# Attention score rows from one stationary block: high and low weights side by side, their two groups of rows added afterwards

## The reference

```
feats   = x W                       (8 heads of 64 units)
e_self  = feats . a_self            e_neigh = feats . a_neigh      (per head and node)
dense   = leaky_relu(e_self[i] + e_neigh[j], 0.2), only where adj[i, j] = 1
x1      = layernorm(x + relu(softmax(dense) feats + b))
agg     = adj x1 / max(row sum of adj, 1e-6)
out     = layernorm(x1 + relu([x1, agg] W1^T))
```

## Time and profile before

| what | us |
|---|---|
| median of 3 runs | 3260.62 (3256.3 to 3260.65) |
| the profiled execution | 3259.45 |
| its span, first to last instruction | 3257.7 |
| TensorE busy (matmul) | 3198.1, 98% of the span |
| VectorE busy | 2351.7, 72% |
| ScalarE busy | 2095.9, 64% |
| GpSimd busy | 283.6, 9% |

### The profile page before, as it was taken

How to read it: one execution, slowest core, us unless ns; L and a number is a source line. 1 busy time by engine, 2 the same in 40 slices (tenths; PEclk the granted TensorE clock), 3 DMA queues, 4 the chain that set the end, 5 groups by cost and what they waited for, 6 DMA issues and landing times.

```text
span 3257.7 us, 124901 instructions
## 1 busy us (share of the span) xinstructions
PE 3198.1 (98%) x56896; PEld 2698.7 (83%) x56896; DVE 2351.7 (72%) x4272; ACT 2095.9 (64%) x2712; POOL 283.6 (9%) x251
## 2 busy tenths in 40 slices
PE   7999999999999999999999999999999999999998
PEld 6969789697896978979788797987969879697895
DVE  6858678586785857859588585876858768586685
ACT  5748567485674947749477494765837658485583
POOL 0010200102011020100202002020020200202001
PEclk8999999999999999999999999999999999999999
DMA  6143151431524225251242513415144251331512
GB/s 217 58 114 102 51 159 66 109 98 51 154 68 118 87 60 157 62 133 65 78 141 63 140 56 94 129 58 146 51 102 120 58 147 62 102 115 51 140 33 49
DMA packets 368657, 314.52 MB, mean 97 GB/s; under 512 B 285056, under 2 KB 285056, under 8 KB 368128
## 3 DMA queue, kind: packets, MB, share of 16 engines
q1 hardware_dynamic: 368128, 306.52, 33.8%
HBM read 205.26 MB, written 34.08 MB: 73 GB/s over the span
## 4 chain that ended last, share of the span: by engine, by line
PE 89%; DVE 6%; issue 2%; ACT 2%; DMA 1%; SPq 0%; DVEq 0%; POOL 0%; ACTq 0%
PE six L940 77%; PE pair L940 11%; DVE mask L769 2%; PE six L964 1%; DVE rest L674 1%; PE pair L964 1%; DVE x_parts L669 1%; ACT step L512 1%; DMA s_bc<-self_scores 1%; ACT trh L477 0%; DVE x_parts L697 0%; DVE trl L708 0%; DMA self_scores<-sc_row 0%; DVE feat L699 0%; DVE trl L905 0%
## 5 line engine op out<-in xcount | busy, mean ns | idle before, releaser
L940 PE MATMUL six<-rows_bf,mask 128*128 128x65 bf16 x45056 | 1507.8, 193 | 19.3 <-DVE mask L769 12.6
L940 PEld LDWEIGHTS six<-rows_bf,mask 128*128 128x128 fp8e4 x45056 | 1497.6, 97 | 27.5 <-DVE mask L769 16.0
L512 ACT ACTIVATE step<-s_bc,n_step 128x1024 uint16<-128x1024 f32 x1024 | 1090.3, 1136 | 90.7 <-DVE mask L769 71.3
L769 DVE TENSOR_TENSOR mask<-adj_t,step 128x1024 uint16<-128x1024 uint16 x1024 | 655.2, 685 | 47.9 <-ACT step L512 47.4
L940 PE MATMUL six<-adj_t,x_parts 128*128 128x512 fp8e4 x1536 | 385.5, 380 | 11.1 <-DVE trl L905 5.4
L455 POOL TENSOR_TENSOR s_bc<-feat,rden 128x512 f32<-128x512 f32 x112 | 124.1, 1113 | 2721.3 <-DVE s_bc L818 2707.1
L940 PEld LDWEIGHTS six<-adj_t,x_parts 128*128 128x128 f16 x1536 | 145.9, 98 | 201.5 <-DVE trl L905 13.2
L477 ACT ACTIVATE mask<-six,rdeg 128x512 f32<-128x512 f32 x128 | 87.9, 686 | 237.5 <-PE six L940 237.5
L940 PE MATMUL six<-w1h,trh 128*128 128x512 f32 x512 | 211.6, 413 | 0.0
L477 ACT ACTIVATE trh<-six 128x512 fp32r<-128x512 f32 x160 | 87.9, 598 | 184.5 <-PE six L940 162.4
L940 PE MATMUL six<-w1h,trl 128*128 128x512 f32 x512 | 201.0, 392 | 0.0
(11 more groups left out here) (127 smaller groups left out, 4922.8 us busy)
## 6 DMA issues: line engine op xcount, KB each, us to landing
s_bc<-self_scores SPq DMA_DIRECT2D x128, 512.0 KB, 3.8
mask<-in_adj_dram SPq DMA_DIRECT2D x64, 512.0 KB, 4.1
adj_nat<-in_adj_dram SPq DMA_DIRECT2D x64, 512.0 KB, 3.5
xs<-in_x_dram SPq DMA_DIRECT2D x128, 256.0 KB, 3.9
out_dram<-mask SPq DMA_DIRECT2D x128, 256.0 KB, 3.3
adj_nat<-in_x_dram SPq DMA_DIRECT2D x64, 256.0 KB, 5.8
step<-in_x_dram SPq DMA_DIRECT2D x64, 256.0 KB, 4.2
xs<-in_L_gnn_W_dram SPq DMA_DIRECT2D x1, 2048.0 KB, 13.2
```

Of the source, the lines that this page charges most:

```text
L512: act.activation(step[:, g % STEP_SLOTS], s_bc[:, h % 2], ACT.Sigmoid, scale=STEP, bias=n_step[:, jt, h:h + 1]).then_inc(stepped.sem, 1)
L769: dve.tensor_tensor(mask[:, g % MASK_SLOTS], adj_t[:, jt, :], step[:, g % STEP_SLOTS], ALU.logical_shift_left).then_inc(masked.sem, 1)
L940: return pe.matmul(o, l, r, start=start, stop=stop, skip_group_check=True)
```

## The change

The high and the low weights of a chunk come to stand in one stationary block: 64 columns apart from chunk to chunk, high in columns 0 to 15, low in columns 32 to 47. One matmul with `trh` and one with `trl` replace the three of before, and PSUM rows 0 to 15 hold the high sums, rows 32 to 47 the low ones (with low x low, which was left out before). ScalarE copies the low rows to a new tile `sc_low`. VectorE adds them to the high rows in PSUM and writes `sc_row`. `sc_f32` is now counted up by that add. In VectorE's order the add of each half stands right in front of the maximum of that half.

```
-        wah_wide = sb("wah_wide", [P, (KC - 1) * SC + P], F32R)
-        wal_wide = sb("wal_wide", [P, (KC - 1) * SC + P], F32R)
-        wah, wal = (w[:, 0:KC * SC].rearrange("p (c n) -> p c n", c=KC) for w in (wah_wide, wal_wide))
+        wa_wide = sb("wa_wide", [P, (KC - 1) * WIDE + P], F32R)
+        wah, wal = (wa_wide[:, 0:KC * WIDE].rearrange("p (c n) -> p c n", c=KC)[:, :, at:at + SC] for at in (0, LOW_ROWS))
...
-            def score_rows(b, i):
+            def score_low_rows(b, i):
                 act.wait_ge(sc_ps.sem, sc_ps.at(b, i + 1))
-                half = slice(i * HALF * P, (i + 1) * HALF * P)
-                copy(sc_row[:, half], bank[SC_BANKS[i]][0:SC, :]).then_inc(sc_f32.sem, 1)
+                if i or b:
+                    act.wait_ge(sc_f32.sem, sc_f32.at(b, 1) if i else sc_f32.at(b - 1, 2))
+                copy(sc_low[:], bank[SC_BANKS[i]][LOW_ROWS:LOW_ROWS + SC, :]).then_inc(sc_low_ok.sem, 1)
...
+            def score_rows(b, i):
+                dve.wait_ge(sc_low_ok.sem, sc_low_ok.at(b, i + 1))
+                half = slice(i * HALF * P, (i + 1) * HALF * P)
+                dve.tensor_tensor(sc_row[:, half], bank[SC_BANKS[i]][0:SC, :], sc_low[:], ALU.add).then_inc(sc_f32.sem, 1)
+
             def first_maximum(b):
+                score_rows(b, 0)
                 dve.wait_ge(sc_f32.sem, sc_f32.at(b, 1))
...
+                score_rows(b, 1)
                 dve.wait_ge(sc_f32.sem, sc_f32.at(b, 2))
                 dve.tensor_reduce(nmax16[:, 1:2], sc_row[:, HALF * P:N], AX.X, ALU.max).then_inc(chain.sem, tick())
...
             def scores(b, i):
                 pe.wait_ge(xt_lo.sem, xt_lo.at(b, (i + 1) * HALF))
-                split_product(bank[SC_BANKS[i]][:], [wah_wide[:, k * SC:k * SC + P] for k in range(KC)],
-                              [wal_wide[:, k * SC:k * SC + P] for k in range(KC)],
-                              [trh[:, k, :] for k in range(KC)],
-                              [trl[:, k, :] for k in range(KC)]).then_inc(sc_ps.sem, 1)
+                for k in range(KC):
+                    for part, rows_of in enumerate((trh, trl)):
+                        ins = mm(bank[SC_BANKS[i]][:], wa_wide[:, k * WIDE:k * WIDE + P], rows_of[:, k, :],
+                                 k == 0 and part == 0, k == KC - 1 and part == 1)
+                ins.then_inc(sc_ps.sem, 1)
```

More of the change, by code:

```diff
@@ L53, in gat_sage_kernel @@
     BANK = 512
+    WIDE, LOW_ROWS = 64, 32
     TPB = BANK // P
@@ L139, in gat_sage_kernel @@
         sc_row = sb("sc_row", [SC, N], F32)
+        sc_low = sb("sc_low", [SC, HALF * P], F32)
         s_bc = sb("s_bc", [P, 2, N], F32)
@@ L237, in gat_sage_kernel @@
         sc_ps = signal("sc_ps", 2)
+        sc_low_ok = signal("sc_low_ok", 2)
         sc_f32 = signal("sc_f32", 2)
@@ L303, in col @@
             return slice(c * P, (c + 1) * P)
-        N_CONST = 6
+        N_CONST = 5
         block = ctx.enter_context(nc.Block())
@@ L447, in _ @@
             pool.memset(eps[:, 1:2], LN_EPS * X1_SCALE ** 2).then_inc(consts, 1)
-            pool.memset(wah_wide[:].bitcast(F32), 0.0).then_inc(consts, 1)
-            pool.memset(wal_wide[:].bitcast(F32), 0.0).then_inc(consts, 1)
+            pool.memset(wa_wide[:].bitcast(F32), 0.0).then_inc(consts, 1)
             for b in range(B):
@@ L528, in weight_exp @@
                     act.activation(o, a[:], ACT.Exp, scale=k).then_inc(weights.sem, 1)
-                score_rows(b, 1)
+                score_low_rows(b, 1)
                 weight_exp(key_w[:, 0], dn, 1.0)
@@ L568, in batch @@
                     if more and t == 1:
-                        score_rows(b + 1, 0)
+                        score_low_rows(b + 1, 0)
                     if t == 5:
@@ L619, in _ @@
                 adj_words(0, t)
-            score_rows(0, 0)
+            score_low_rows(0, 0)
             act.wait_ge(ft_ps.sem, ft_ps.at(0, HALF))
```

## The result

| | before | after |
|---|---|---|
| median | 3260.6 us (5 runs) | 3276.4 us (3273.0 to 3280.5, 5 runs) |
| ratio of the runs, 95% interval | 1 | 1.0052 (1.0041 to 1.0062) |
| the profiled execution, its span | 3259.5, 3257.7 | 3276.6, 3274.8 |
| TensorE busy | 3198.1 | 3181.2 |
| TensorE's granted clock, mean | 0.997 | 0.990 |

What follows compares the result with a forecast made beforehand. TensorE held 89% of the chain, but at seams between batches the first mask word, through the scores' load, governed. -13.9 + 6.0 + 0.5 = -7.4 us gave 3252.0, set at 3252.5 us; own range 3246 to 3254, with rivals to 3264.

Steps and rivals of the forecast that it cites:

- The store of the scores: At the seam between batches: issued 1.22 us later in the mean, but taking 1.84 us to land instead of 2.68.
- The mask word: VectorE's first of a batch, said to govern the batch through the load of the scores; that load 0.40 us later.
- The transposes: TensorE's score-row transposes at the seam: 0.47 to 0.93 us late behind the add, mean 0.68, within slack.
- rival 2: Score store has a floor of 2.0 to 2.2 us: delay 0.55 to 0.74 us, 3254 to 3257 us; chance 0.25.
- Rival 1: Score store isn't quicker: issued and landing 1.22 us later, +4.9 us, 3264.3 us; chance 0.13.
- The seam has two times that matter: the arrival of TensorE (slack): Between two batches: TensorE has over half a microsecond to spare; the landing of the score store has none.
- So the 0.93 us arrive at the next seam: 15 x 0.93 = 13.9 us gained: First `scores` call of a batch: four matmuls fewer save 0.93 us, all kept to the next batch boundary.
- the wait of `own(0)`: After the first call: TensorE's need for normalised parts has 3.3 us of room against 0.68 + 0.93 = 1.6.
- rival 4: First call's gain doesn't arrive: normalisation, 0.68 us later, holds the aggregation; +6.5 us, 3266 us; chance 0.05.
- +6.0: Cost in us over 15 seams of the load of the scores coming 0.40 us later at each.
- the start, +0.5: Batch 0: the add costs 0.70 us in the chain, the second call's store is 0.23 us earlier; together +0.5 us.
- Rival 3: TensorE's 0.68 us lateness at the transposes isn't slack but reaches the heads' end: -3.3 us, 3256 us; chance 0.07.

Runs made afterwards that it cites:

- experiment 1: The changed kernel plus six matmuls with unused sums before the transposes at every seam between batches: 3264.9 us, ratio 1.0012.
- Experiment 2: The changed kernel with the first half's maximum moved to the end of the layer norm, its add staying in place: 3264.1 us, ratio 1.0011.
- experiment 3: The changed kernel with the seam's add in front of VectorE's last normalisation of the batch, not behind it: 3258.6 us, ratio 0.9991.
- experiment 4: The changed kernel with the seam's add ahead of the last normalisation and the first half's maximum later: 3247.9 us, ratio 0.9956.
- 8: The kernel before, its seam transposes also waiting for feature tile 4, with five unused matmuls ahead of that wait: 3268.4 us, ratio 1.0032.
- experiment 12: The kernel before, with the store of y tile 6 and load of x tile 7 issued behind the score store: 3253.8 us, ratio 0.9981.

## Why the prediction was wrong

*The store of the scores: right.* I took 1.84 us for a store without the traffic ahead and had 1.46 to 2.20 as bounds; it is 1.63 (1.48 to 1.85). The mask word is 0.23 us later in the mean, where I had 0.40. The transposes are 0.59 us later, where I had 0.68. I had set the 2.0 us of the Trainium skill ("DMA: Bandwidth & Descriptors", Anatomy of one DMA) beside it. That section fits them to DMAs issued by GpSimd, and this store is issued by SyncE; it took 0.37 us less in the mean, and no run shows the 2.0 us as a floor for it (rival 2). Rival 1 falls.

*The failed step, and the larger: "The seam has two times that matter: the arrival of TensorE (slack)".* I priced TensorE's wait by its length alone, 0.68 us in a slack of over 0.5, at nothing. (The rows that I showed had 0.53 us of slack, less than 0.68. That the slack is wide enough was luck: with the filler the same lateness cost 0.1 us.) I named the idle time (1.4 us, measured 1.77 in the mean) and didn't ask what a TensorE that stands does to its own clock, though every comparison of key tiles and mask words came from seams with a clock of 1.00. In place of slack stand 9.67 us for work of 8.19. Within the changed kernel's trace, the 11 batches with the half clock behind the seam have 99.07 us from mask word to first call, the 3 without 97.82. 12 x 1.25 = 15 us would be the loss. But two of the 11 (100.31 and 101.16 us) also hold 1.8 and 2.5 us of idle time that the profile puts to no cause, and the other nine have 98.69: 12 x 0.87 = 10 us. The filler of experiment 1 gave 11.4 back, so the clock cost some 10 to 15 us.

*The second failed step: "So the 0.93 us arrive at the next seam: 15 x 0.93 = 13.9 us gained".* 0.25 arrived, 3.7 us in all. I held the 0.68 us of the add against the wait of `own(0)`, with 3.3 us of room, and overlooked an earlier one, for the feature rows of tiles 0 and 1. In the kernel before that wait had 0.3 us of room, and 0.68 later plus 0.93 earlier is more: TensorE now waits 0.69 us there, which leaves 0.24 of the 0.93. So rival 4 was right in kind, but its place was another: not the x1 parts, but the feature rows. Experiment 2 gives the 0.93 back.

*The sum.* -13.9 became -3.7, +6.0 became +3.4, and the 10 to 15 us for the clock were not in it at all; nor were the 4.2 us of the last batch, and the start, +0.5, became -1.1. Rival 3 had the right engine and place, but lateness was not what cost, and its price of 0.68 us for each seam was too low.

*What stays open:* why the clock fell behind 12 seams of 15 after 1.77 us of idle time, behind 11 and 10 after 1.1 and 1.0, and behind 3 after 1.5 in the kernel before with a wait. Behind the seams with 0.61 us or less in front of the transposes in experiments 1, 3, 4 and 8 it fell once in 59 (in experiment 4, where 0.57 us more stood in front of the product of the maximum). So idle time matters, but its length alone doesn't say whether the clock falls.

## What to carry to other kernels

Idle time of a busy TensorE isn't free even in front of slack: look at the granted clock behind every new wait, and fill the wait with work of its own before you judge a change. An operation moved to another engine takes on the queue of that engine: the add is 0.67 us, its place behind the landing of an unrelated store was the cost, and one position further ahead it made no loss that shows (experiment 3). Where a gain of an engine is to arrive at a later point, list every wait between the two, and take the tightest.

## What the runs showed that I had not expected

- A store of 16 KB took 1.47 to 1.50 us from issue to the load behind it with little ahead of it (experiment 12), and 2.20 to 3.35 us in the kernel before, behind two stores of 256 KB, a load and a transpose. Its issue on SyncE then grew too, from 0.30 to as much as 1.16 us in experiment 4.
- Six matmuls of 512 columns whose sums nobody reads, at each of 16 seams, made the changed kernel 11.4 us faster.
- The add of 16 partitions took 0.67 us, as a sum over 128 partitions does, and ScalarE's copy from PSUM rows 32 to 47 to SBUF partitions 0 to 15 took 0.59, as the one without a shift.
